# A transformer kernel on one core: the lead-in of the block-product QKV stage re-ordered on every engine, and the late rows' operands spread over the projection

## The reference

```python
query = hidden_states @ Wq.T                    # first layer's feed-forward block
...                                             # top 8 of 256 slots, their values down to 64 columns
u = _uncertainty(hidden_states, Wu1, bu1, Wu2, bu2)    # holds a mean over all tokens
u_norm = jnp.clip((u - TAU_LOW) / (TAU_HIGH - TAU_LOW), 0.0, 1.0)
gate = jax.nn.sigmoid(gate_w1 * u_norm + gate_bias)
gate = jnp.where(gate < EARLY_EXIT, 0.0, gate)
hidden = hidden_states + gate[..., None] * aux_out     # aux_out = z @ Wvu.T
x = _layernorm(hidden)
qkv = jnp.einsum('sbh,ph->sbp', x, weight_qkv)         # second layer's attention block
...                                                    # causal attention, 32 query heads, 8 key and value heads
x = _layernorm(x + einsum('sbe,he->sbh', attention, weight_proj))
```

## Time and profile before

| | us |
|---|---|
| median of three runs | 3239.0 |
| lowest and highest of them | 3230.96, 3241.22 |
| the profiled execution's own time | 3240.99 |
| its span, first to last instruction | 3239.0 |
| PE busy, share of the span | 3025.5, 93% |
| DVE busy | 1983.3, 61% |
| ACT busy | 1591.9, 49% |
| POOL busy | 1157.6, 36% |

### The profile page before, as it was taken

The page is one execution under the profiler, slowest core; times in us unless marked ns, Lnnn a source line. Parts: engine busy times, 40 slices in busy tenths (PEclk is TensorE's granted clock), DMA queues, the critical chain, the costliest instruction groups (busy, mean ns, idle before and its releaser), DMA issues. The chain is left out here.

```text
span 3239.0 us, 69982 instructions
## 1 busy us (share of the span) xinstructions
PE 3025.5 (93%) x26232; PEld 2522.1 (78%) x26232; DVE 1983.3 (61%) x4938; ACT 1591.9 (49%) x4162; POOL 1157.6 (36%) x1023
## 2 busy tenths in 40 slices
PE   5999999996699999999989999999999699999997
PEld 3888888874488888788878888888887578888886
DVE  6788888884545455545554444444445588888885
ACT  2777877783432323232323222232222487777774
POOL 2222222212264554454536564555644101111110
PEclk8999999996699999999999999999999799999999
DMA  9777877763012222222254121221211855656651
GB/s 280 188 188 188 198 195 188 192 148 91 20 53 88 79 83 69 76 79 82 87 217 146 63 85 60 72 72 54 85 59 63 270 146 151 151 151 151 151 146 47
DMA packets 234199, 397.96 MB, mean 123 GB/s; under 512 B 32281, under 2 KB 161913, under 8 KB 233354
## 3 DMA queue, kind: packets, MB, share of 16 engines
q1 hardware_dynamic: 230408, 391.29, 43.2%
q10 hardware_dynamic: 3458, 2.20, 0.2%
HBM read 296.98 MB, written 96.43 MB: 121 GB/s over the span
## 5 line engine op out<-in xcount | busy, mean ns | idle before, releaser
L1460 POOL TENSOR_TENSOR sa_r_lo<-sa_raw,sa_r_hi 128x512 fp32r<-128x512 f32 (+1 forms) x304 | 466.1, 1533 | 679.4 <-ACT sa_r_hi L1754 595.5
L756 ACT ACTIVATE L_probs<-L_masked,L_least 112x375 f32<-112x375 f32 x1024 | 628.1, 615 | 79.5 <-DVE L_least L885 75.4
L885 DVE CUSTOM_DVE_ANT_0 L_masked<-L_scores,L_nmask 112x375 f32<-112x375 f32 x1024 | 552.6, 544 | 175.2 <-PE L_scores L489 139.0
L494 PEld LDWEIGHTS L_turned<-ident_sb,L_probs 112*125 112x125 f32 x3072 | 457.1, 189 | 107.0 <-issue 48.1
L494 PE MATMUL L_turned<-ident_sb,L_probs 112*125 112x112 f32 x3072 | 526.3, 280 | 7.1 <-ACT L_probsT L751 3.5
L1597 PE MATMUL sa_banks<-both_hi,sa_r_hi 128*128 128x420 f32 (+1 forms) x1344 | 498.5, 371 | 11.4 <-DVE both_lo L1930 6.6
L1597 PE MATMUL sa_banks<-both_lo,sa_r_hi 128*128 128x420 f32 (+1 forms) x1344 | 490.5, 365 | 0.0
L1597 PE MATMUL sa_banks<-both_hi,sa_r_lo 128*128 128x420 f32 (+1 forms) x1344 | 490.3, 365 | 0.0
L1996 DVE TENSOR_TENSOR sa_acc<-sa_acc,sa_banks 128x512 f32<-128x512 f32 x448 | 304.6, 685 | 246.3 <-PE sa_banks L1656 240.3
L489 PE MATMUL L_scores<-L_krep,L_qrep 128*112 128x376 f32 x1024 | 418.0, 409 | 7.5 <-DMA L_qrep<-query_parts 6.5
L751 ACT COPY L_probsT<-L_turned 125x336 f32<-125x336 f32 x768 | 337.5, 440 | 177.1 <-PE L_turned L494 169.6
(11 more groups left out here) (320 smaller groups left out, 5322.4 us busy)
## 6 DMA issues: line engine op xcount, KB each, us to landing
L_qrep<-query_parts SPq DMA_DIRECT2D x256, 224.0 KB, 6.2
sa_raw<-in_wqkvU_dram SPq DMA_DIRECT2D x192, 256.0 KB, 3.3
L_krep<-ctx_parts SPq DMA_DIRECT2D x256, 188.0 KB, 4.2
sa_raw<-in_wprojU_dram SPq DMA_DIRECT2D x128, 256.0 KB, 3.0
query_parts<-L_qT_hi SPq DMA_DIRECT2D x64, 224.0 KB, 6.4
query_parts<-L_qT_lo SPq DMA_DIRECT2D x64, 224.0 KB, 7.0
L_xcur<-x SPq DMA_DIRECT2D x64, 224.0 KB
L_val<-in_ctx_dram SPq DMA_DIRECT2D x64, 187.5 KB
```

Of the source, the lines that this page charges most:

```text
L494: mm = pe.transpose(turned[0:TC, m % 2, S * j:S * j + S], probs[0:S, m % 4, TC * j:TC * j + TC], ident[0:S, 0:S])
L756: nc.scalar.activation(probs[0:S, e % 4, :], masked[0:S, e % 4, :], ACT.Exp, bias=least[0:S, e:e + 1], scale=-1.0, accum_out=rsum[0:S, e:e ...
L885: v.tensor_tensor_reduce(out=masked[0:S, n % 4, :], in0=scores[0:S, (NH * t + n) % 3, 0:T], in1=nmask[0:S, :], scale=1.0, scalar=HUGE, op0 ...
L1460: p.tensor_tensor(lo, src, hi.bitcast(F32), ALU.subtract).then_inc(done, 1)
```

## The change

- **DVE, lead-in:** row `c` is now `gated_sum(c)`, `moments(c)`, `low_parts(c - 2)`, `differences(c - 1)`. `low_parts` has only the four operands T1, T3, T2 and T4.
- **POOL, lead-in:** the other three low parts (B11, B21, B22) are made by POOL in the new `low_blocks`, with a semaphore of its own (`low_ok`). A root now comes first, then the blocks of the row before it, then one weight step for each of the first four rows.
- **ACT, lead-in:** `norm(c)`, the four high parts of the differences of row `c - 1`, one weight cast in the first four rows, `copy_turned(c)`, the three plain high parts of row `c`.
- **PE, lead-in:** one `take_aux` ahead of the second transpose of z, and then always one row ahead of `turn_row`.
- **SP, lead-in:** Wvu is loaded ahead of the first four pieces of weights, and these stand behind rows 1 and 3.
- **Late rows:** in `accumulate(G, 0)` the two differences move from `c == 0` to `c == 1`, the three low parts from `c == 1` to `c == 3`.

The remaining lines count the semaphores anew, since low parts of half 0 now come from two engines.

```diff
@@ -1153,6 +1153,8 @@
 
     B11, T1, T2, B21, T3, T4, B22 = range(OPS)
     MAKE = (B11, B21, B22, T1, T3, T2, T4)
+    NB = 3
+    NT = OPS - NB
     ROUNDS = ((B11, B21, T1, T2), (B22, T4, T3))
 
     ends_half = lambda G: G % NKV == NKV - 1
...
@@ -1325,7 +1327,9 @@
         block = ctx.enter_context(nc.Block())
 
         EARLY0, EARLY1, STORE0, STORE1 = (NC * i for i in range(4))
-        made = lambda half, c, i: OPS * NC * half + OPS * c + sum(len(x) for x in ROUNDS[:i])
+        made = lambda c, i: OPS * c + sum(len(x) for x in ROUNDS[:i])
+        late_hi = lambda c, i: OPS * NC + made(c, i)
+        late_lo = lambda c, i: NT * NC + made(c, i)
         heads_done = lambda G, hp: 2 * NC * (nth[G, hp] + 1)
 
         @block.sync
@@ -1353,7 +1357,8 @@
                     sp.dma_start(dst[:, j, :], src.bitcast(F32)).then_inc(expert_stored, 16)
 
             def load_late(r):
-                sp.wait_ge(lo_ok, made(1, r, 0))
+                sp.wait_ge(lo_ok, late_lo(r, 0))
+                sp.wait_ge(low_ok, NB * NC)
                 sp.dma_start(late[:], rows[1, r][:, 0:D]).then_inc(ld_late, 16)
 
             def store_late(r):
...
@@ -1381,12 +1386,13 @@
             for dst, src in ((ones, "ones"), (w1[:], "gate_w1"), (gb[:], "gate_bias")):
                 sp.dma_start(dst, io[src]).then_inc(ld_gate, 16)
             sp.dma_start(z, blocks[:, :, D:D + BOT]).then_inc(ld_z, 16)
-            for i in range(4):
-                load_raw(i)
             for h in range(2):
                 sp.dma_start(wvu[BOT * h:BOT * h + BOT, :], io["wvuT"]).then_inc(ld_wvu, 16)
             for c in range(NC):
                 sp.dma_start(acc[:, c, :], rows[0, c][:, 0:D]).then_inc(ld_row_then_x[c], 16)
+                if c in (1, 3):
+                    load_raw(c - 1)
+                    load_raw(c)
             masks = io["causal"].rearrange("(q l b) k -> l q b k", l=2, b=LEN)
             for l in range(2):
                 sp.dma_start(io["causal_t"][:, :, l, :], masks[l]).then_inc(ld_causal, 16)
@@ -1482,6 +1488,12 @@
                     if o in (T3, T4, B22):
                         pool.drain().then_inc(raw_free, 2 if o == T3 else 1)
 
+            def low_blocks(c):
+                for n, o in enumerate(MAKE[:NB]):
+                    pool.wait_ge(hi_ok, OPS * c + n + 1)
+                    hi, lo = operand_place(0, c, o)
+                    p.tensor_tensor(lo, operand_source(0, c, o), hi.bitcast(F32), ALU.subtract).then_inc(low_ok, 1)
+
             def heads(G, hp):
                 hi, lo = heads_of(G, hp)
                 for j in range(2):
@@ -1501,9 +1513,13 @@
 
             p.memset(half_exp[:], -0.5)
             pool.drain()
-            weights(0, KV, 0, RING)
             for c in range(NC):
                 root(EARLY0 + c)
+                if c:
+                    low_blocks(c - 1)
+                if c < RING:
+                    weights(0, KV, c, c + 1)
+            low_blocks(NC - 1)
             weights(0, KV, RING)
             for G in range(GROUPS):
                 if G == NKV:
@@ -1571,7 +1587,11 @@
                 n = OPS * m + o
                 pe.wait_ge(w_ok, n + 1)
                 if m == 0:
-                    pe.wait_ge(lo_ok, OPS * (NC - 1) + MAKE.index(o) + 1)
+                    n_made = MAKE.index(o)
+                    if n_made < NB:
+                        pe.wait_ge(low_ok, NB * (NC - 1) + n_made + 1)
+                    else:
+                        pe.wait_ge(lo_ok, NT * (NC - 1) + n_made - NB + 1)
                 if (G, pr) == (NKV, KV):
                     pe.wait_ge(ld_row_then_x[o], 16 + 32)
                 if o == B11 and m:
@@ -1664,14 +1684,13 @@
             pe.matmul(banks[:, 3, 0:1], ones, lsum[:], start=True, stop=True).then_inc(mean_ok, 1)
             pe.wait_ge(ld_z, 16)
             turn_z(0)
+            pe.wait_ge(ld_wvu, 32)
+            take_aux(0, 0)
             turn_z(1)
-            pe.wait_ge(ld_wvu, 32)
-            for c in range(3):
-                take_aux(0, c)
             for c in range(NC):
+                if c + 1 < NC:
+                    take_aux(0, c + 1)
                 turn_row(0, c, acc[:, c, :])
-                if c + 3 < NC:
-                    take_aux(0, c + 3)
 
             for G in range(GROUPS):
                 r = late_row(G)
@@ -1712,7 +1731,8 @@
                 if half:
                     act.wait_ge(late_stored, 16 * (c + 1))
                 elif c >= 2:
-                    act.wait_ge(lo_ok, OPS * (c - 1))
+                    act.wait_ge(lo_ok, NT * (c - 1))
+                    act.wait_ge(low_ok, NB * (c - 1))
                 for h in range(2):
                     out = ring[:, slot["turn", c, h][0], :] if half else banks[:, 2 * (c % 2) + h, :]
                     whole = qT[:].rearrange("p j t -> p (j t)")[:, 0:D] if half == 0 and c % 2 else late[:]
@@ -1724,9 +1744,9 @@
 
             def high_parts(half, c, i=0):
                 if half and (c or i):
-                    act.wait_ge(part_stored, 2 * 16 * (made(1, c, i) - made(1, 0, 0)))
+                    act.wait_ge(part_stored, 2 * 16 * made(c, i))
                 n = 0
-                for o in (MAKE if half == 0 else ROUNDS[i]):
+                for o in ((MAKE[:NB], MAKE[NB:])[i] if half == 0 else ROUNDS[i]):
                     if o in (T1, T2, T3, T4):
                         n += 1
                         act.wait_ge(diff_ok, 4 * (NC * half + c) + (2 * i if half else 0) + n)
...
@@ -1845,17 +1865,15 @@
             act.wait_ge(arg_gate, 1)
             nc.scalar.activation(t_g[:], u_g[:], ACT.Tanh, scale=0.5).then_inc(tanh2_ok, 1)
             take_z(1)
-            for n in range(RING):
-                cast_weight(n)
             for c in range(NC):
-                if c > 1:
-                    high_parts(0, c - 2)
                 norm(EARLY0 + c, acc[:, c, :], norm_ok)
                 if c:
-                    copy_turned(0, c - 1)
-            copy_turned(0, NC - 1)
-            for c in range(NC - 2, NC):
-                high_parts(0, c)
+                    high_parts(0, c - 1, 1)
+                if c < RING:
+                    cast_weight(c)
+                copy_turned(0, c)
+                high_parts(0, c, 0)
+            high_parts(0, NC - 1, 1)
             for G in range(GROUPS):
                 r = late_row(G)
                 for o in range(OPS):
@@ -1924,8 +1942,8 @@
                 dve.drain()
 
             def low_parts(half, c, i=0):
-                for n, o in enumerate(MAKE if half == 0 else ROUNDS[i]):
-                    dve.wait_ge(hi_ok, (made(half, c, i) if half else OPS * c) + n + 1)
+                for n, o in enumerate(ROUNDS[i] if half else MAKE[NB:]):
+                    dve.wait_ge(hi_ok, (late_hi(c, i) if half else OPS * c + NB) + n + 1)
                     hi, lo = operand_place(half, c, o)
                     v.tensor_tensor(lo, operand_source(half, c, o), hi.bitcast(F32), ALU.subtract).then_inc(lo_ok, 1)
 
@@ -2000,9 +2018,9 @@
                     if c % 2 == 0:
                         for later in range(c + 2, min(c + 4, NC)):
                             low_weighted(G, hp, later)
-                    if hp == 0 and c == 0 and late_row(G) is not None:
+                    if hp == 0 and c == 1 and late_row(G) is not None:
                         differences(1, late_row(G), 1)
-                    if hp == 0 and c == 1 and late_row(G) is not None:
+                    if hp == 0 and c == 3 and late_row(G) is not None:
                         low_parts(1, late_row(G), 1)
                     if ends_half(G) and hp == 0 and c == 0:
                         softmax_scale(G, 1)
@@ -2040,16 +2058,16 @@
             dve.drain()
 
             for c in range(NC):
-                if c >= 2:
-                    differences(0, c - 2)
                 gated_sum(0, c, acc[:, c, :])
                 moments(EARLY0 + c, acc[:, c, :])
                 if c >= 2:
                     low_parts(0, c - 2)
-            for c in range(NC - 2, NC):
-                differences(0, c)
-                low_parts(0, c)
-            dve.wait_ge(hi_ok, OPS * NC)
+                if c:
+                    differences(0, c - 1)
+            low_parts(0, NC - 2)
+            differences(0, NC - 1)
+            low_parts(0, NC - 1)
+            dve.wait_ge(low_ok, NB * NC)
             v.memset(qT[:].rearrange("p j (m t) -> p (j m) t", t=32)[:, :, 0:FIRSTS], 0.0)
             dve.wait_ge(ld_causal, 32 + 16)
             v.tensor_copy(causal[:].rearrange("p (b l) -> p b l", l=2), mask_in.rearrange("p (l b) -> p b l", l=2))
```

6 lines of the change are left out of this document (3 added, 3 removed).

## The result

| | before | after | predicted |
|---|---|---|---|
| median, us | 3239.5 | 3215.7 | 3218 (3208 to 3231) |
| lowest and highest | 3230.96, 3241.22 | 3213.59, 3223.08 | |
| profiled execution | 3240.99 | 3215.61 | 3220.2 |

After to before is 0.9936, with a 95% interval from 0.9920 to 0.9951: 0.6% faster, clear of the scatter, and within the predicted range.

A forecast was written before the change was run, and what follows sets the result against it. Lead-in bound by a chain across engines, the stretch behind it by PE. Gains 1.0 + 10.0 + 3.8 = 14.8 there and 6.0 in late rows: 3241.0 - 14.8 - 6.0 = 3220.2 profiled, 3218 as median, range 3208 to 3231.

The forecast's parts named there:

- First rows: Start of the lead-in: with Wvu loaded first, norm 1 comes at 810.5 instead of 811.50, a gain of 1.0 us.
- Rows between: Lead-in, rows 1 to 6: five rows take 39.2 us against 49.24, a gain of 10.0 us.
- The loop is broken: Lead-in: gated_sum(c) no longer waits for a copy of row c - 1, out of a loop of 9.5 us.
- Port waits: Lead-in: DVE operations with two SBUF inputs wait until POOL's end, taken as about 1 us a row.
- The slower rival: Lead-in: each of DVE's eight two-input operations waits for a whole POOL instruction, 15 us a row; 3254, chance 0.03.
- The end: Lead-in, last norm to first block product: 6.1 us instead of 9.89, a gain of 3.8 us.
- Late rows (5.4 + 0.6): Groups 1 to 6: six waits of 1.7 us go, 0.8 of stall each stays, 5.4; group 7's wait of 0.60 goes.
- SP's later issue: Late rows: SP loads the next row some 4 us later; the 5.3 us left before its sum cover the load.
- no change: Lead-in: DVE's and ACT's lists lock again, a row takes 9 us, only start and end gain; 3236, chance 0.09.
- the small case: Lead-in gains only 8 us (POOL's blocks cost 1.26, weights land late), late rows 1; 3230, chance 0.2.

The follow-up runs named there:

- the split: Changed kernel with the two late-row differences apart: T4 at c == 1, T3 ahead of the small low parts of c == 2; 3214.8 us, ratio to before 0.992.
- the one beside it: Changed kernel with all seven low parts of the early rows made by DVE, none by GpSimd; 3218.7 us, ratio to before 0.991.

## Why the prediction was right, step by step

- **First rows (1.0).** Mis-sized. Norm 1 stood 18.5 us behind the first matmul and stands at 16.1: 2.4. The fourth piece of weights, which I had landing at 806 by sizes, was there at 803.17, which is 805.1 on the old clock of the stage, and POOL had waited only 1.49 for it. The run with the old start says 2.7 to 3.2 for the start as a whole.
- **Rows between (10.0).** 49.24 - 39.05 = 10.2, right in the sum, and less so in its parts: 8.9, 7.3, 7.3, 8.3, 7.3 where I had 10.3, 6.1, 8.0, 7.4, 7.4. A row has a floor of 7.25, DVE's list, which is what rows without a weight step take (norms 7.25 apart from row 2 on with the old start). I had it for the last rows only, so 6.1 was too low, and I charged the first weight step too much. The 8.3 comes from row 3's weight step lying beside DVE's low parts: three of them take 1.79 (the fence of DVE's row above) and not 1.04. "The loop is broken" was right; the reason given was wrong. "`gated_sum(c)` no longer waits for a copy of row c - 1": it never did, and it waits for the copy of row c - 2 as before. ACT's place for that copy breaks the loop. So the sum of the rows owes something to luck: the reason as given doesn't ask for ACT's new list, and without that list they take 51.4.
- **Port waits (1 us a row).** Right in size and in kind. In the changed kernel's lead-in 19 two-input operations of DVE on SBUF took longer than 0.43, most of them 0.78 to 0.95, and every one ends 0.28 or 0.29 us behind an instruction of POOL; the same holds in the other traces, and before, with no such work of POOL beside them, none is longer than 0.43. So DVE's instruction is held until POOL's is over. That costs what POOL's has left: 0.35 to 0.6 each beside the blocks, two or three times a row, and 1.1 each beside two of the weight steps, where low parts took 1.49 and 1.50. POOL is held as well: its second and third block end 0.59 behind DVE's instruction and take 0.9, where they take 0.7 alone and I took 0.66. The slower rival, eight whole ones a row, was far from it, since only the operations that meet a block are held. What I had not said is that these waits eat up nearly all of what sharing saves in a row. The Trainium skill, "SBUF — State Buffer", section "Who interferes with whom", has the later of the two blocked until the other's instruction is over, and the traces agree, by the 0.28 above.
- **The end (3.8).** 9.89 - 5.98 = 3.9. The second product followed without a wait, as said.
- **Late rows (5.4 + 0.6).** The six waits: 5.3, with 0.8 left each as taken. Their cause, the two differences in one piece, is shown by the split. The step that failed is group 7: "the wait of 0.60 goes too". It has 0.61 + 0.78 instead, 0.8 more. By the code DVE has the second half's softmax between the same additions in that group, and I had not laid the two side by side; that this is the cause was not tried. Nor are the 0.8 surely the edit's: behind its first wait of 2.3, group 7 has 0.60 in one trace of before and 2.7 in the other, 0.75 to 1.4 in the four of the changed kernel.
- **SP's later issue.** The next late row was issued at 1029.01 and its sum began at 1034.41, which gives 5.4 us (5.3 predicted), and the sum waited for PE and not for it.
- **Not foreseen:** the earlier start, 2.0, the matmul pace, 5.6, and one idle time of 2.2 in the profiled execution. (The first product, forecast between 854 and 858, came at 852.19, which is 854.2 on the old clock of the stage.) They aren't shown to be part of the change; the lead-in, the six waits and group 7 alone give 16.5 + 5.3 - 0.8 = 21.0, and I had 20.8. That these two agree so well is luck: the lead-in gave 1.7 more than I had, the late rows 1.5 less. The scatter of the other waits (3.0) and the clock (3.3) took back more than half of what start, pace and idle time had brought.
- **A sum among the rivals:** "no change", 3236, leaves out the late rows' 6.0, which come there too. With them it is 3230, near the small case, and those two couldn't have been told apart by the time.

## What to carry to other kernels

When several engines run the same rows in a chain, look for the instruction that stands in a list behind the *next* row's wait: moving that one (here ACT's copy) is worth more than dividing work, and a list off that loop may not matter. Before a loop is called re-ordered, write out both lists: here DVE's, which I had thought changed, was the same. Work handed from DVE to GpSimd saves nothing in a row if its operations lie beside DVE's two-input ones; put it where DVE waits. And before a few tenths of a per cent are credited to an edit, compare a stretch that it doesn't touch.

## What the runs showed of the hardware

PE's clock can fall behind a stall of under 2 us. In the kernel with the late edit undone, behind the wait of 1.80 us that ended at 1017.46 (columns: length, PE busy, PEclk, DMA share, GB/s):

```profile
1017.50:1019.00 1.50, 1.50 (x7) 0.99 0.00 0
1019.00:1022.40 3.40, 3.40 (x23) 0.50 0.36 120
1022.40:1030.00 7.60, 7.60 (x46) 1.00 0.58 188
```

For 3.4 us the clock stands at 1.2 GHz, with PE busy throughout, which costs half of that, 1.7 us, on top of the stall (an estimate from the two clocks). In the 14 traces, between 900 and 1630 us, there are 24 waits for an addition that took 1.78 us or more, and 11 of them have such a stretch (one of 6.8 us, behind the longest wait), beginning within 1.6 us of the wait's end; the 144 others, of up to 1.77 us, have none. So a stall of 1.8 us can cost 3.5. The kernel with the late edit undone has three of these stretches, the other kernels at most one each. That may be why it lies 7.9 us above the one beside it, where the six waits alone explain 5.3.
